# Cross-attention with an fp4 feed-forward on one core: four scalings move from VectorE to GpSimd, and the events of a batch get new places

## What is computed

```python
def fp4_quant_dequant(x):                      # blocks of 16 along the last axis
    scale = max(max|xb| / 6, 1e-12); xn = xb / scale
    return _GRID[searchsorted(_MID, |xn|)] * sign(xn) * scale      # grid 0 .5 1 1.5 2 3 4 6
def fp4_linear(x, w): return fp4_quant_dequant(x) @ fp4_quant_dequant(w).T

xn = layernorm(x)                                                  # first norm
Q, K, V = heads(xn @ Wq), heads(ctx @ Wk), heads(ctx @ Wv)
x  = x + merge(softmax(Q K^T / 4) V) @ Wo + bo
xn = layernorm(x)                                                  # second norm
h  = silu(fp4_linear(xn, w_gate)) * fp4_linear(xn, w_up)           # 704 wide
x  = x + fp4_linear(h, w_down)
```

## Time and profile before

| | |
|---|---|
| median of 3 runs | 3553.26 us (3552.5 to 3557.31) |
| profiled execution | 3561.53 us, its span 3559.8 us |
| mean granted clock of PE | 0.945 |
| busy: PE, DVE, ACT, POOL | 94%, 81%, 63%, 20% |
| chain that ended last: PE, DVE, ACT | 79%, 11%, 4% |

### The profile page before, as it was taken

How to read it: one execution, slowest core, us unless ns; L and a number is a source line. 1 busy time by engine, 2 the same in 40 slices (tenths; PEclk the granted TensorE clock), 3 DMA queues, 4 the chain that set the end, 5 groups by cost and what they waited for, 6 DMA issues and landing times.

```text
span 3559.8 us, 55150 instructions
## 1 busy us (share of the span) xinstructions
PE 3335.2 (94%) x19606; PEld 1692.0 (48%) x19606; DVE 2874.6 (81%) x6429; ACT 2254.1 (63%) x4512; POOL 696.0 (20%) x796
## 2 busy tenths in 40 slices
...
GB/s 89 53 51 48 34 54 53 34 67 34 44 47 50 51 44 46 35 56 54 34 67 31 44 47 45 57 45 46 34 57 53 35 66 24 47 53 36 42 19 8
DMA packets 120777, 163.24 MB, mean 46 GB/s; under 512 B 47125, under 2 KB 93606, under 8 KB 120506
## 3 DMA queue, kind: packets, MB, share of 16 engines
...
## 4 chain that ended last, share of the span: by engine, by line
PE 79%; DVE 11%; ACT 4%; SPq 2%; DMA 2%; issue 1%; POOL 0%; DVEq 0%; POOLq 0%
PE out_ps L990 19%; PE ring L1004 15%; PE ring L977 15%; PE ring L940 7%; DVE piece_max L1336 6%; PE ring L951 5%; PE ring L915 4%; PE ring L907 4%; ACT probs L1106 3%; PE ring L931 2%; SPq L796 2%; PE ring L948 2%; DMA q_stack<-neg_rows 2%; PE ring L925 1%; PE ring L896 1%
## 5 line engine op out<-in xcount | busy, mean ns | idle before, releaser
L1336 DVE TENSOR_REDUCE piece_max<-ring 128x1 f32<-128x402 f32 x4096 | 2069.7, 567 | 303.2 <-PE ring L1004 291.2
L1106 ACT ACTIVATE probs<-ring 128x512 f32<-128x512 f32 (+1 forms) x3328 | 1794.6, 600 | 696.7 <-PE ring L977 677.8
L1004 PE MATMUL ring<-k_stack,q_stack 48*128 48x402 f32 x4096 | 886.0, 406 | 50.6 <-DVE piece_max L1336 34.0
L990 PE MATMUL out_ps<-probs,v_ones 128*17 128x512 f32 x6656 | 921.3, 627 | 1.4 <-ACT probs L1106 1.4
L977 PE MATMUL ring<-q_stack,k_stack 50*128 50x512 f32 (+1 forms) x3328 | 844.9, 474 | 46.9 <-DMA q_stack<-neg_rows 36.2
L977 PEld LDWEIGHTS ring<-q_stack,k_stack 50*128 50x128 f32 (+1 forms) x3328 | 350.7, 187 | 881.0 <-issue 277.3
L1004 PEld LDWEIGHTS ring<-k_stack,q_stack 48*128 48x128 f32 x4096 | 468.9, 196 | 321.3 <-DVE piece_max L1336 177.6
L1384 POOL TENSOR_TENSOR h<-h,h_grid 128x704 f32<-128x704 f32 (+1 forms) x68 | 101.3, 1489 | 1176.2 <-DVE h_grid L1169 1176.2
L940 PE MATMUL ring<-wgu_T,xq_T 128*128 128x512 f32 (+1 forms) x1080 | 250.4, 383 | 1.8
L990 PEld LDWEIGHTS out_ps<-probs,v_ones 128*17 128x17 f32 x6656 | 111.4, 96 | 233.9 <-issue 199.8
L940 PEld LDWEIGHTS ring<-wgu_T,xq_T 128*128 128x128 f32 x1080 | 193.9, 188 | 52.5 <-issue 21.4
...
## 6 DMA issues: line engine op xcount, KB each, us to landing
k_stack<-k_parts SPq DMA_DIRECT2D x256, 200.1 KB, 4.5
k_stack<-k_parts SPq DMA_DIRECT2D x256, 100.1 KB, 4.3
...
q_stack<-q_parts SPq DMA_DIRECT2D x256, 64.0 KB, 2.3
...
q_stack<-q_parts SPq DMA_DIRECT2D x256, 32.0 KB, 2.0
...
```

What stands on the lines that cost most here:

```text
L990: last = pe.matmul(out_ps[32 * j:32 * j + V1, :], v_ones[0:r, batch % 2, m, PER_GROUP * g + j, :], probs[0:r, step % 2, j, :], start=(m == ...
L1004: pe.matmul(ring[:, bank(kind, batch, item), 0:PW], q_stack[rows, at, t * P:(t + 1) * P], k_stack[rows, at, a:b], start=True, stop=True).t ...
L1106: act.activation(probs[0:r, step % 2, j:j + n, :], ring[0:r, at:at + n, :], ACT.Exp, scale=SCORE_SCALE).then_inc(probs_ready, n)
L1336: dve.tensor_reduce(piece_max[:, j:j + many, t, c], ring[:, at:at + many, 0:PW], AX_X, ALU.max).then_inc(pieces_max, many)
```

## The change

Four things that DVE did in the body batches go to POOL: `ln1_apply`, `ln2_apply`, and `fp4_scale` for xq and for h (event `xq_max` now ends with POOL's scaling; `xq_scale` keeps DVE's `fp4_grid` and POOL's rounding). DVE's `h_grid` and `xq_scale` wait for POOL's product by the same semaphores as before for its own. The prologue's first norm, the weights of batch 0 and the whole tail stay on DVE.

```diff
+            def fp4_scale(src, inverse, done, base):
+                pool.wait_ge(done, base(3))
+                pool.tensor_scalar(src, src, BELOW_TIE, 1.0, ALU.mult, ALU.mult).then_inc(scaled, 1)
+                pool.wait_ge(scaled, scale_number[0])
+                scale_number[0] += 1
+                pool.tensor_tensor(fp4_blocks(src), fp4_blocks(src), over_block(inverse, src.shape[1] // BLOCK), ALU.mult).then_inc(done, 1)
...
+                elif name == "ln1_apply" and kind != "start":
+                    pool.tensor_scalar(mean_var[:, :, 0], mean_var[:, :, 0], -1.0, 1.0, ALU.mult, ALU.mult).then_inc(ln1_neg, 1)
+                    pool.wait_ge(ln1_neg, nxt)
+                    pool.wait_ge(ln1_rstd, count(nxt, 2, 2))
+                    for t in range(QT):
+                        last = pool.tensor_scalar(x_in[:, t, :], x_in[:, t, :], mean_var[:, t, 0:1], rstd[:, t:t + 1], ALU.add, ALU.mult)
+                    last.then_inc(ln1_step, 1)
...
+                elif name == "ln2_apply" and kind != "tail":
...
+                    if t or old:
+                        pool.wait_ge(*(drained(kind, batch, ("xq_T", t - 1)) if t else drained(*body_before(kind, batch), ("xq_T", QT - 1))))
+                    pool.tensor_scalar(q.xq, x1_of(kind, t), q.mean_var[:, 0:1], q.rstd, ALU.add, ALU.mult).then_inc(ln2_step, 1)
+                elif name == "xq_max" and kind != "tail":
...
+                    fp4_scale(q.xq, q.xq_small[:, 0, :], xq_step, lambda k: count(old, ROUNDING * QT, ROUNDING * t + k))
+                elif name == "h_scale" and kind != "tail":
...
+                    fp4_scale(q.h, q.h_small[:, 0, :], h_step, lambda k: count(old, ROUNDING * QT, ROUNDING * t + k))
```

The places. Most move by one to five halves of a step:

```diff
 POST_AT = [
-    [4, 5, 5, 9, 13, 14, 19, 20, 20, 21, 23, 23, 23, 26, 33, 34, 38],
-    [22, 23, 23, 23, 32, 37, 38, 43, 45, 45, 48, 48, 51, 51, 56, 62, 65],
-    [52, 55, 55, 58, 59, 59, 65, 66, 66, 66, 68, 69, 70, 73, 78, 80, 85],
-    [74, 74, 74, 74, 74, 78, 82, 86, 86, 87, 87, 93, 95, 95, 100, 101, 102],
+    [4, 5, 13, 13, 15, 16, 19, 20, 21, 21, 23, 23, 23, 26, 36, 37, 41],
+    [17, 23, 23, 23, 32, 37, 41, 43, 45, 45, 48, 48, 51, 51, 56, 62, 65],
+    [54, 57, 57, 58, 58, 59, 65, 66, 66, 66, 67, 69, 70, 73, 78, 80, 85],
+    [69, 74, 74, 75, 77, 79, 85, 86, 86, 86, 86, 89, 93, 95, 100, 101, 102],
 ]
...
-PRE_AT = [26, 28, 29, 30, 37, 37, 47, 48, 51, 51, 54, 55, 59, 62, 66, 69, 69, 70, 78, 83, 87, 91]
+PRE_AT = [27, 28, 32, 32, 37, 37, 47, 48, 52, 52, 53, 53, 59, 62, 66, 71, 71, 72, 78, 83, 87, 95]
...
-LN1 = 6
+LN1 = 9
...
 PIECES_AT = [
-    [3, 3, 4, 3, 2, 3, 3, 3, 3, 3, 2, 0, 0],
-    [3, 3, 3, 2, 3, 3, 4, 3, 3, 3, 2, 0, 0],
-    [3, 3, 3, 2, 3, 3, 3, 3, 3, 3, 3, 0, 0],
-    [3, 3, 4, 4, 4, 1, 3, 3, 2, 3, 2, 0, 0],
+    [3, 3, 4, 4, 0, 3, 4, 3, 4, 3, 1, 0, 0],
+    [3, 3, 3, 1, 3, 4, 3, 4, 4, 3, 1, 0, 0],
+    [3, 2, 4, 1, 1, 4, 4, 4, 1, 5, 3, 0, 0],
+    [4, 3, 4, 4, 4, 1, 1, 3, 3, 3, 2, 0, 0],
 ]
-STEP_ORDER = "S01 P W01 P S23 P V"
+STEP_ORDERS = ['S01 P W P S23 P V', 'S01 P W P S23 P V', 'S01 P W P S23 P V', 'S01 P W P S23 P V', 'S01 P W P S23 P V', 'S01 P W P S23 P V', 'S01 P W P S23 P V', 'S01 P W P S23 P V', 'S01 P W P S23 P V', 'S01 P W P S23 P V', 'S01 P W P S23 P V W', 'S01 P W P S23 P V', 'S01 P W P S23 P V']
+PROB_SLOTS = 8
+DRAIN_AFTER = {}
```

More of the change, by code:

```diff
@@ L258, in build, with ring_of @@
     BANKS = sum(RINGS)
-    RING_OF = {"scores": RING_FOR[0], "piece": RING_FOR[1], "round": RING_FOR[2]}
+    def ring_of(kind, item):
+        return RING_FOR[0 if item[0] == "scores" else 1 if item[0] == "piece" else 3 if by_vector(kind, item[1]) else 2]
+    VALUES_LEFT = STEPS
+    for step in range(STEPS):
+        ready = step - (STEPS - VALUES_LEFT)
+        VALUES_LEFT -= min(STEP_ORDERS[step % KEY_TILES].split().count("V"), ready)
     def transposes(event):
@@ L320, in sequence @@
         if kind == "tail":
-            put(0, "weighted", -1)
+            for n in range(VALUES_LEFT):
+                put(0, "weighted", n - VALUES_LEFT)
             for _, es in sorted(EVENTS[kind].items()):
@@ L326, in sequence, with put_events @@
             return seq
+        value = 0 if kind == "first" else -VALUES_LEFT
+        pending = sorted(EVENTS[kind].items())
+        def put_events(until):
+            while pending and pending[0][0] <= until:
+                for e in pending.pop(0)[1]:
+                    put(0, "event", e)
+                    put_rounds([e])
         for g in range(PHASES):
@@ L332, in sequence @@
                 step = g * KEY_TILES + m
-                left, slots = ahead * 2 * PIECES_AT[g][m], STEP_ORDER.count("P")
-                for what in STEP_ORDER.split():
+                left, slots = ahead * 2 * PIECES_AT[g][m], STEP_ORDERS[m].count("P")
+                for what in STEP_ORDERS[m].split():
                     if what == "P":
@@ L343, in sequence @@
                             put(NQ, "scores", step, int(j))
-                    elif what[0] == "W":
-                        for part in what[1:]:
-                            for e in EVENTS[kind].get(2 * step + int(part), []):
-                                put(0, "event", e)
-                                put_rounds([e])
-                    elif step or kind != "first":
-                        put(4 * NQ, "weighted", step - 1)
+                    elif what == "W":
+                        put_events(2 * step + 1)
+                    elif value < step:
+                        put(4 * NQ, "weighted", value)
+                        value += 1
+        put_events(2 * STEPS)
         return seq
@@ L360, in pair_slot, with prob, prob_slot @@
         return pair(batch, g, u) % PAIR_SLOTS
+    def prob(batch, step, j):
+        return (batch * STEPS + step) * PER_GROUP + j
+    def prob_slot(batch, step, j):
+        return prob(batch, step, j) % PROB_SLOTS
     def stacked_until(k):
@@ L430, in bank_user @@
         return kind, batch, BANK_USERS[kind][of][n]
-    def partner(item):
-        return item[:-1] + (item[-1] + 1,)
-    PLACE = {k: {item: n for n, item in enumerate(SEQUENCE[k])} for k in SEQUENCE}
-    def merged(kind, batch, item):
-        if not MERGE[("scores", "piece").index(item[0])] or item[-1] % 2:
-            return False
-        at = PLACE[kind]
-        return at.get(partner(item)) == at[item] + 1 and bank(kind, batch, partner(item)) == bank(kind, batch, item) + 1
-    def follows(kind, batch, item):
-        return item[-1] % 2 == 1 and merged(kind, batch, item[:-1] + (item[-1] - 1,))
     ctx = ExitStack()
@@ L662, in at_step @@
             if step < 0:
-                return batch - 1, PHASES - 1, KEY_TILES - 1
+                return batch - 1, PHASES - 1, KEY_TILES + step
             return (batch,) + divmod(step, KEY_TILES)
@@ L1190, in handle @@
                     last.then_inc(ln1_step, 1)
-                elif name == "ln1_apply":
+                elif name == "ln1_apply" and kind == "start":
                     dve.wait_ge(ln1_rstd, count(nxt, 2, 2))
@@ L1265, in handle @@
                     dve.bn_aggr(q.mean_var, q.stats).then_inc(ln2_step, 1)
-                elif name == "ln2_apply":
+                elif name == "ln2_apply" and kind == "tail":
                     t = event[1]
```

73 lines of the change are left out of this document (40 added, 33 removed), and 4 rows, old and new, of the table TAIL_AT.

## The result

The changed kernel takes 3445.2 us (median of 4 runs, 3434.9 to 3455.6) against 3555.3 for the kernel before; the ratio is 0.9685, 95% interval 0.9647 to 0.9723. That is 110 us less, where 80 were forecast.

What follows compares the result with a forecast made beforehand. PE and DVE were taken to bound in turns, DVE in steps full of pieces, PE in steps full of projections. 5.9 + 1.0 - 1.6 = 5.3 us per batch, 15 batches, 80 us, gave 3473 us; range 3425 to 3540.

Steps and rivals of the forecast that it cites:

- DVE's relief: Scalings and norms leaving DVE: of 8.5 us a batch, the 5.9 us among pieces count whole.
- Moves: Heads' transposes, out_proj's cover and last context transposes change steps: together 1.0 us a batch gained, shift rows' wait growing 0.4.
- Shared ports: DVE's short instructions shut out while POOL runs, through ports shared with GpSimd: 1.6 us a batch lost.
- two more meetings: Two more short DVE instructions a batch, of 32 exposed, held up by a POOL instruction, up to 0.8 us each.
- Waits of DVE for POOL, set against each other: DVE's new waits for h and xq on POOL balanced against its ended 28.0 us wait for the norm's reciprocal root.
- The clock, taken as unchanged: Sum of 5.3 us per batch held no term for the granted clock; its cases stood only inside the range.
- rival 4: Batches of 211.9 and 215.0 us differ by clock alone: 3426 or 3520 us, inside the forecast, 0.72 with its clock cases.
- Rival 1: Hidden anyway: PE bounds also among pieces, only its visible idle time shrinks, some 1 us a batch, 3538 us; chance 0.12.
- Rivals 2 and 3: 2: shared ports lengthen 16 DVE conversions, 6 us more per batch, 3645, chance 0.08; 3: DVE waits for POOL, 3755, 0.04.
- POOL's sum: POOL's added work per batch for h, xq and both norms: 23.1 us, or 10.7 with the lower end; no bound.

Runs made afterwards that it cites:

- e1_work_only: The changed kernel with all tables of places and pieces of the kernel before, so only the work moves to POOL; 3476.5 us, 0.9783 of the kernel before.
- e7: The changed kernel with the scaling of xq back on DVE; 3436.6 us, 0.9660 of the kernel before.
- e12: The changed kernel with two more products with 1.0 on POOL in each scaling of h; 3442.0 us, 0.9688 of the kernel before.

## Why the prediction was right, and which terms were off

The forecast of 3473 with 3425 to 3540 held, but its terms were wrong in opposite directions, and that they nearly cancel is luck. Term by term:

- *DVE's relief, 5.9 us a batch.* The step that failed is to take 5.9 us whole because they lie among pieces. In the old places e1_work_only shows 2.3 us at full clock, and only in steps where PE stood idle. That run's total, 80 us, came out above the 65 expected because 3.2 us a batch of it are the clock. In the new places the parts are worth more: h in quarters 2 and 3 1.1 (1.8 forecast), xq 1.0 (0.4 net of the wait), the first norm 2.0 (1.6), the second at most 0.6 (0.8), together with 0.1 for the two scalings in steps without pieces 4.8. That work counts among pieces and not elsewhere held.
- *Moves, 1.0.* The waits before the heads' transposes and out_proj went where forecast. The wait for the shift rows grew by 1.0 us instead of 0.4, and the 0.9 us of step 13 had no term. What the places are worth at full clock alone is not settled: 208.3 is only an upper bound.
- *Shared ports, 1.6 lost.* Nothing was lost. The step that failed is "I take two more meetings": the long cases of line 1248 and the mean of the conversions stayed where they were. It took conversions as exposed that never met POOL, and POOL's new work ran beside reductions of pieces, which kept their 567 ns.
- *Waits of DVE for POOL, set against each other.* They rose from the 28.0 us of the earlier trace rows to 29.2 + 27.8 + 20.7 = 77.7 in the run. The 20.7 cost nothing, as e7 shows, and doubling the 27.8 cost at most 0.3 us a batch in e12. What the 29.2, in steps 37 and 38, cost was not taken apart.
- *The clock, taken as unchanged.* This term was mis-sized, and it makes up the missing 30 us. Time at 1.2 GHz fell from 15.8 to 7.4 us a batch. A batch became 214.2 - 207.0 = 7.2 us shorter, of which 3.1 us is the clock by the corrected value and 2.0 by the upper bound; 15 batches at 2.0 to 3.1 are 30 to 47 us. I had listed it as rival 4 and left it within the range.

At full clock 5.3 us were forecast and 4.1 measured, 5.2 by the upper bound.

Rival 1 (hidden anyway) falls in its number, 3538. Its mechanism is what the old places show, where only PE's visible idle time shrank, though by 2.3 us instead of 1. In the new places it fails too, since h's scaling costs 0.3 us in step 35 and 0.5 in step 47 with no idle time of PE. Rivals 2 and 3 fall with e12. POOL's sum in the prediction has two slips that nothing rests on: its prices add up to 23.2 and not 23.1, and with the lower end for every one-input instruction to 12.1 and not 10.7.
